# Scaling the attention probabilities: all four tiles of a step on ScalarE instead of two on GpSimd and two on ScalarE

## The reference

```python
x = x + tanh(g_xattn) * xattn(ctx, layernorm(x))     # x (16,256,256), ctx (16,77,256)
x = x + tanh(g_ffn) * ffn(layernorm(x))              # 15 experts, top 2, plus a shared expert with a causal conv

# inside xattn: 16 heads of 64, keys = context rows and latent rows together (77 + 256 = 333)
q = l @ Wq ; kv = concat([x, l]) @ Wkv ; k, v = split(kv)
w = softmax(einsum('bhqd,bhkd->bhqk', q * scale, k * scale))
out = einsum('bhqk,bhkd->bhqd', w, v) @ Wo
```

## Time and profile before

| | before |
|---|---|
| median of 3 runs | 1304.1 us (1301.31 to 1305.29) |
| the profiled execution's own time | 1300.85 us |
| its span, first to last instruction | 1299.1 us |
| TensorE busy | 1233.8 us (95%) |
| VectorE busy | 880.0 us (68%) |
| ScalarE busy | 787.4 us (61%) |
| GpSimd busy | 460.1 us (35%) |
| mean granted TensorE clock | 0.991 |

### The profile page before, as it was taken

One profiled execution on the slowest core, in us unless ns is written; L12 is line 12 of the kernel. 1 busy time (PEld: TensorE's weight loads), 2 busy tenths in 40 slices (PEclk: granted clock), 3 DMA queues, 4 the chain that ended last, 5 costly groups with the idle time before them and its releaser, 6 DMA issues.

```text
span 1299.1 us, 28231 instructions
## 1 busy us (share of the span) xinstructions
PE 1233.8 (95%) x8982; PEld 1014.8 (78%) x8982; DVE 880.0 (68%) x2646; ACT 787.4 (61%) x2278; POOL 460.1 (35%) x638
## 2 busy tenths in 40 slices
PE   3899999999999999999999999999999989999996
PEld 2788888888887888788878887888888868887774
DVE  5676677777777777777777777777776645444554
ACT  2766666666666666566656665666666666444442
POOL 2422323333333333333333333333423222444554
PEclk9999999999999999999999999999999999999998
DMA  8910000000000000000000000000000151445666
GB/s 253 314 51 2 3 2 3 18 4 17 4 18 5 17 12 10 10 14 12 10 10 13 12 10 14 10 12 10 9 10 14 44 160 45 120 130 169 195 207 211
DMA packets 61839, 70.90 MB, mean 55 GB/s; under 512 B 7072, under 2 KB 56176, under 8 KB 61680
## 3 DMA queue, kind: packets, MB, share of 16 engines
q1 hardware_dynamic: 54192, 48.91, 13.1%
q0 software_dynamic: 6912, 18.95, 4.1%
q10 hardware_dynamic: 576, 1.05, 0.2%
HBM read 35.19 MB, written 33.70 MB: 53 GB/s over the span
## 4 chain that ended last, share of the span: by engine, by line
PE 89%; DVE 5%; issue 2%; ACT 2%; DMA 1%; POOL 1%; DVEq 0%; SPq 0%; POOLq 0%; ACTq 0%
PE pj L1358 28%; PE ov L1423 14%; PE st L1388 11%; PE st L1404 11%; PE yb L1484 6%; PE st L560 5%; PE pj L513 3%; PE ov L579 3%; DVE PT L1342 2%; PE st L550 2%; PE pj L516 1%; PE ov L1013 1%; PE yb L527 1%; PE st L572 1%; ACT K_hl L1181 1%
## 5 line engine op out<-in xcount | busy, mean ns | idle before, releaser
L1161 ACT ACTIVATE probs<-st,neg_max 128x333 f32<-128x333 f32 x512 | 268.8, 538 | 266.8 <-DVE neg_max L1309 238.4
L1106 POOL TENSOR_TENSOR probs<-probs,inv_sum 128x333 f32<-128x333 f32 x128 | 94.7, 740 | 654.3 <-DVE inv_sum L1320 654.3
L1309 DVE TENSOR_REDUCE neg_max<-st 128x2 f32<-128x666 f32 x256 | 205.8, 845 | 130.4 <-PE st L1404 130.4
L1423 PE MATMUL ov<-PT,V 128*64 128x256 f32 (+1 forms) x1536 | 197.8, 393 | 0.0
L1388 PE MATMUL st<-ident,probs 128*128 128x128 f32 (+1 forms) x1536 | 189.0, 272 | 0.2 <-ACT probs L1161 0.2
L1388 PEld LDWEIGHTS st<-ident,probs 128*128 128x128 f32 (+1 forms) x1536 | 176.2, 143 | 3.4 <-issue 0.8
L1404 PE MATMUL st<-K_hl,Q_hl 64*128 64x334 f32 x1536 | 152.5, 330 | 15.5 <-issue 9.5
L1342 DVE COPY PT<-st 128x512 f32<-128x512 f32 x256 | 163.7, 681 | 0.0
L1358 PE MATMUL pj<-wkv,lT 128*128 128x512 f32 (+1 forms) x576 | 158.4, 410 | 3.9 <-DVE Q_hl L1324 3.8
L1423 PEld LDWEIGHTS ov<-PT,V 128*64 128x64 f32 (+1 forms) x1536 | 100.3, 138 | 64.6 <-issue 28.4
L1404 PEld LDWEIGHTS st<-K_hl,Q_hl 64*128 64x128 f32 x1536 | 117.7, 186 | 34.5 <-issue 19.7
(11 more groups left out here) (177 smaller groups left out, 1801.1 us busy)
## 6 DMA issues: line engine op xcount, KB each, us to landing
slots_x<-zeros SPq DMA_DIRECT2D x10, 1032.0 KB, 13.8
V<-slots_x SPq DMA_DIRECT2D x80, 129.0 KB
yg<-routed_y SPq DMA_DIRECT2D x32, 256.0 KB
out<-X SPq DMA_DIRECT2D x32, 128.0 KB
X<-in_x SPq DMA_DIRECT2D x2, 1024.0 KB, 13.9
w_gu<-in_L_ffn_expert_gate_w SPq DMA_DIRECT2D x2, 960.0 KB, 8.6
w_gu<-in_L_ffn_expert_up_w SPq DMA_DIRECT2D x2, 960.0 KB, 10.3
w_dn<-in_L_ffn_expert_down_w SPq DMA_DIRECT2D x1, 1920.0 KB, 13.7
```

What stands on the lines that cost most here:

```text
L1106: pool.tensor_tensor(probs[:, v, 0, 0:SKV], probs[:, v, 0, 0:SKV], inv_sum[:, v, 0:1].to_broadcast([P, SKV]), ALU.mult).then_inc(normed, 1)
L1161: nc.scalar.activation(probs[:, v, i, 0:SKV], st_bank(i)[:, 0:SKV], ACT.Exp, bias=neg_max[:, v, i:i + 1], accum_out=sums[:, v, i:i + 1]).t ...
L1309: nc.vector.tensor_reduce(neg_max[:, v, 2 * i:2 * i + 2], st[i][:, :, 0:SKV], AX.X, ALU.max, negate=True).then_inc(maxed, 1)
L1423: last = mm(ov[half * HALF:(half + 1) * HALF, 0:SQ], V[0:kn, kt, head * DH:(head + 1) * DH], PT[0:kn, v, kt, half * SQ:(half + 1) * SQ], s ...
```

## The change

GpSimd's two scaling instructions of a step are gone. ScalarE scales all four tiles, at the same place of its order, behind its copy of the keys and ahead of its copy of the third transposed bank. The two semaphores become one with four counts a step, and TensorE's transposes wait for that one.

```diff
@@ gpsimd step
-            if has(LAG_S):
-                m, v = PAIRS * bb + u - LAG_S, (u - LAG_S) % 2
-                pool.wait_ge(inv_ready, m + 1)
-                pool.tensor_tensor(probs[:, v, 0, 0:SKV], probs[:, v, 0, 0:SKV],
-                                   inv_sum[:, v, 0:1].to_broadcast([P, SKV]), ALU.mult).then_inc(normed, 1)
-                for i in range(1, 2):
-                    pool.tensor_scalar(probs[:, v, i, 0:SKV], probs[:, v, i, 0:SKV],
-                                       inv_sum[:, v, i:i + 1], None, ALU.mult).then_inc(normed, 1)
@@ scalar step
                 act.wait_ge(inv_ready, m + 1)
-                for i in range(2, 4):
+                for i in range(0, 4):
                     copy(probs[:, v, i, 0:SKV], probs[:, v, i, 0:SKV], ACT.Copy,
-                         scale=inv_sum[:, v, i:i + 1]).then_inc(normed_too, 1)
+                         scale=inv_sum[:, v, i:i + 1]).then_inc(normed, 1)
@@ tensor step
-                pe.wait_ge(normed, 2 * (PAIRS * bb + u - LAG_T + 1))
-                pe.wait_ge(normed_too, 2 * (PAIRS * bb + u - LAG_T + 1))
+                pe.wait_ge(normed, 4 * (PAIRS * bb + u - LAG_T + 1))
```

More of the change, by code:

```diff
@@ L721, in attention @@
     normed = sem("normed")
-    normed_too = sem("normed_too")
     pt_full = sem("pt_full")
```

## The result

| | before | after |
|---|---|---|
| median | 1302.7 us (4 runs, 1299.69 to 1305.29; one more than in the part before) | 1316.24 us (4 runs, 1314.65 to 1316.47) |
| profiled execution, span | 1300.85, 1299.1 us | 1316.24, 1314.5 us |
| granted TensorE clock in it | 0.991 | 0.986 |

The ratio is 1.0097, 95% interval 1.0076 to 1.0117: the change costs 13.5 us, where 12.8 was forecast. The same changed kernel, run again in a later series, gave 1316.16 us (six runs) and 1.0101 [1.0082, 1.012].

What follows compares the result with a forecast made beforehand. TensorE bounds the kernel, paying only where ScalarE's later copy into PT delays it. Terms 8.2 + 2.0 + 1.4 (steps 3 and 11) + 0.6 + 0.6 = 12.8 us on 1304.1 gave 1316.9 us; range 1308 to 1325.

Steps and rivals of the forecast that it cites:

- What bounds the kernel: TensorE, busy 95% of the span; ScalarE's 72% decides nothing, only whether its copy into PT delays the next scores.
- The term of p = 7: Steps 7, 15, ..., 127: scores wait 0.68 us more for ScalarE's copy into PT; 12 paying places, 8.2 us.
- p = 3: Steps with the router's small matmuls instead of the V projection: 0.14 us each in 14 steps, 2.0 us.
- Steps with V: The other six p, with a V projection: the copy ends 1.73 us before the scores, so they pay nothing.
- The loop's pauses: Four p = 7 steps at the loop's branch back, TensorE idle 2.37 us anyway: they pay nothing.
- Step 2 and the end: Step 2, late through the copies of Wo, and the expert part's rows after attention: 0.6 us later each.
- What is removed: GpSimd's 740 + 1129 ns a step and VectorE's 18.4 us of scatter waits: their removal gains 0 us.
- Rival 3: Longer pauses before the scores lower TensorE's clock, 1.6 us a time: 22 us more, 1339 us; chance 7%.

Runs made afterwards that it cites:

- GpSimd silent: Kernel before, without GpSimd's two scalings and TensorE's wait for them, two tiles left unscaled: 1302.8 us, ratio 0.9999.
- two with swapped copies: Kernel before; in p = 3 and 7 ScalarE's two scalings go behind its copy into PT, and it takes one VectorE copy: 1299.83 us, 0.9974.
- four swapped: Changed kernel; in p = 3 and 7 ScalarE's four scalings go behind its copy into PT, and it takes one VectorE copy: 1300.42 us, 0.9984.
- five: Changed kernel with a fifth scaling, into an unread spare buffer, ahead of ScalarE's copy into PT: 1329.9 us, ratio 1.0208.
- two extra scalings: Kernel before, GpSimd's scalings kept, with two more ScalarE scalings into an unread buffer ahead of its copy into PT: 1314.19 us, 1.0082.

## Why the prediction was right

**What bounds the kernel.** Right. ScalarE's 68% of the span said nothing; the distance between its copy into PT and the next scores said all. The kernel with the scalings moved last shows it most plainly, with the same scalings on the same engine and a sixth of the cost.

**The term of p = 7**. Right in mechanism and count, 0.64 us instead of 0.68. The copy into PT started 2.20 us after that of K (467.25 - 465.05) instead of 1.31, so 0.89 later and not 0.96: four scalings took 467.25 - 465.39 = 1.86 us, 0.465 each. The 0.96 for two in the earlier trace rows was misread as the price of two scalings. Its last distance ends at the copy into PT, and that copy had waited for the transposes, which end at 459.15 (the line in the section on the result). The prediction said that the copy had no idle time to hide anything in; it had 0.04 us. So these 0.04 us count twice in the 0.07: once in the price of two scalings (0.93 by the distances in the four), once as time that was free. The kernel with the scalings last shows this wait alone: there the copy into PT starts 1.31 us after that of K as well (460.46 - 459.15), with no scaling between them. Against the shorter delay, the scores start 0.15 us after ScalarE's copy, where the prediction took VectorE's 0.10. Less 0.07 for the delay, plus 0.05 for the hand-over, less 0.02 for a copy of 0.57 instead of 0.59 make the 0.04 that is missing. The prediction's estimate from the Trainium skill's page "ScalarE: Activation LUTs", section "What ACT_TABLE_LOAD costs", was 0.46 a piece, and this trace agrees with 0.465.

**p = 3**. Right: 0.11 for 0.14. The copy had ended 0.92 us ahead of the scores, so of the delay of 0.89 us all but the last 0.11 was free.

**Steps with V**. Right, nothing; and the fifth scaling shows that this cover was close to its end in p = 0 and p = 2, where less was left than in the row shown.

**The loop's pauses**. That the copy pays nothing there held. But the pauses themselves were 2.36 to 2.78 us in this profile and 2.36 to 2.39 before, 0.8 us more in all. With GpSimd silent, where the copies stand as before, they were 2.52 to 2.76, so this is not shown to come from the change.

**Step 2 and the end**. Right, 0.61 and 0.5 for 0.6 and 0.6.

**What is removed**. Right, nothing: the silent GpSimd shows it for the scalings and the ports. VectorE's waits for the scatter mostly went, from 18.4 us in 14 waits to 4.1 us in 2, and the steps of p = 3 got no shorter by it.

**The clock.** This is the part the sum left out. The 12.8 were 1.4 too high by the steps, and the median came out 13.5 over before, with 1.5 to 1.8 us that go with the lower clock on top. The two errors nearly cancel, and that the total came so close is luck. Rival 3 named the mechanism, at the loop's pauses, but not its first place: the pause ahead of step 3 went from 1.94 to 2.57 us, and in this profile a stretch at 1.2 GHz follows it. The pauses of 0.93 us in steps 3, 11 and those of p = 7, on which the rival's 22 us rested, were followed by the full clock in both profiles of the changed kernel.

That step 3's stretch belongs to the change is likely, and not shown. With pauses of at most 2.1 us ahead of step 3 (before, GpSimd silent, three scalings, the scalings last, two with swapped copies) none followed. With pauses of 2.55 us or more it followed in the changed kernel, in its repetition, with four swapped and with five, but not with two extra scalings nor with the scalings behind the copy in p = 3 and 7. Each of these is one profiled execution. Nor is step 3 the whole of it: with three scalings on ScalarE it kept the full clock, and still those runs had a mean clock of 0.9874 against 0.9893. With five scalings and the longest pauses of all, the mean clock was that of before (0.9896). So how much of the clock's part is the change's stays open.

The end of attention is a second place. In the changed kernel the pause of 1.96 us there was followed by half clock, in before that of 1.45 was not; but with GpSimd silent a pause of 1.44 was:

```profile
1042.74 1.06 PE L503 MATMUL pj<-ident,h_row 128*128 128x128 f32 x4 [1.44 <-ACT h_row L331]
1043.73 2.75 PE L1415 MATMUL ov<-PT,V 128*64 128x256 f32 x12
```

## What to carry to other kernels

Moving work to an engine that is at 61% is priced by its place in that engine's order: for each step, the time added ahead of the next thing that the bounding engine waits for, minus the distance from the end of that thing to the moment it is used, and plus the hand-over. Where that thing had itself waited for another engine, take off that wait as well (here 0.04 us). Steps of one loop can have very different distances (here 0.38 us in p = 7, 0.92 in p = 3, and 1.4 or more with a V projection), so read one timeline of each kind and count them. If the work must move, put it behind the hand-over: here 2 to 3 us instead of 13.5, and with one copy shifted to the engine that is then early, no loss at all. Then look for what else waits on that engine: behind the scalings the copy into `w_cv` cost 0.7 us, and the expert part's rows 1.0.

## What the runs showed of the hardware that was not expected

- From the end of a copy to the matmul that waits for it, 0.14 to 0.15 us pass where the copy is ScalarE's (changed, two extra, five) and 0.10 or less where it is VectorE's (and 0.05 with ScalarE's scalings last).
- TensorE's clock after a pause, in the steps of attention: after 0.93 to 1.40 us it was full each time, after 1.93 to 2.10 us ahead of step 3 it was full in the five kernels that had it. After the loop's pauses of 2.35 to 2.88 us it fell to half in 40 of 48 cases over twelve profiles, which cost 1.4 to 1.6 us in most. In three of them it stayed low for longer: the step behind the branch took 10.66 us in the repeated changed kernel (step 80), against 7.80 at the full clock and 9.4 otherwise.
- The length of the pause doesn't decide alone. The same pause of 2.36 to 2.39 us was followed by both in one profile, the full clock followed one of 2.78 us (five, step 64), and at the end of attention half clock followed one of 1.44 us (GpSimd silent).
- A loop's pause is not of fixed length in this kernel: 2.36 to 2.39 us in the four of before, 2.35 to 2.88 over all profiles.
